# A transformer layer on one core: another order around the last heads, the shared expert and the second batch's first steps

## The reference

```python
x = x + attention(layernorm(x))        # 16 heads, 128 + 64 rotary features per head,
                                       # keys and values from a normed latent of 64
x = x + moe(layernorm(x))              # 8 experts of width 176, each token goes to its top 2;
                                       # beside them a shared expert of width 352
def moe(x):
    scores = softmax(x @ gate_w)                       # decides the experts of a token
    routed = sum over the top 2 of score * (silu(x @ w_gate) * (x @ w_up)) @ w_down
    shared = (silu(x @ sw_gate) * (x @ sw_up)) @ sw_down
    return routed + shared
```

## Time and profile before

| | |
|---|---|
| median of 3 executions | 633.29 us (632.36 to 633.71) |
| the profiled execution | 640.3 us, span 638.6 us |
| TensorE busy | 611.4 us (96%) |
| VectorE busy | 469.9 us (74%) |
| ScalarE busy | 474.8 us (74%) |
| GpSimd busy | 410.1 us (64%) |
| mean granted TensorE clock | 0.974 |

### The profile page before, as it was taken

The page is one execution under the profiler, slowest core; times in us unless marked ns, Lnnn a source line. Parts: engine busy times, 40 slices in busy tenths (PEclk is TensorE's granted clock), DMA queues, the critical chain, the costliest instruction groups (busy, mean ns, idle before and its releaser), DMA issues. The chain is left out here.

```text
span 638.6 us, 15728 instructions
## 1 busy us (share of the span) xinstructions
PE 611.4 (96%) x4916; PEld 596.4 (93%) x4916; DVE 469.9 (74%) x1406; ACT 474.8 (74%) x1331; POOL 410.1 (64%) x455
## 2 busy tenths in 40 slices
PE   9988999999999999999999999999988889999995
PEld 8878999999999999899999999999978879999994
DVE  6666787877886888778688788778755666666486
ACT  4669899898998989779898898979854335565531
POOL 1466797786897889679789988978603204444500
PEclk9997999999999999999999999999989689999997
DMA  9891000000001001000100100011403055444292
GB/s 254 254 332 29 2 1 3 2 2 34 10 10 42 10 18 44 8 16 5 43 18 10 43 9 19 34 53 43 149 1 133 33 152 166 131 119 133 77 316 87
DMA packets 34024, 45.41 MB, mean 71 GB/s; under 512 B 4056, under 2 KB 29112, under 8 KB 33944
## 3 DMA queue, kind: packets, MB, share of 16 engines
q1 hardware_dynamic: 29160, 34.56, 17.2%
q0 software_dynamic: 3408, 9.34, 4.5%
q10 hardware_dynamic: 1376, 0.50, 0.3%
HBM read 27.57 MB, written 16.82 MB: 70 GB/s over the span
## 5 line engine op out<-in xcount | busy, mean ns | idle before, releaser
L1244 ACT ACTIVATE probs<-ps_s,nmax 128x256 f32<-128x256 f32 x256 | 118.9, 475 | 14.4 <-DVE nmax L1434 14.3
L1779 POOL TENSOR_TENSOR qswap<-qswap,qsin 128x512 f32<-128x512 f32 x64 | 83.2, 1300 | 45.6 <-ACT qswap L1221 45.6
L226 PE MATMUL ps_q<-xa,wq_hi 128*128 128x256 f32 x512 | 101.0, 295 | 4.3 <-DVE qf L1429 4.3
L1434 DVE TENSOR_REDUCE nmax<-ps_s 128x2 f32<-128x512 f32 x128 | 86.9, 679 | 11.1 <-PE ps_s L226 10.6
L1221 ACT ACTIVATE pT_hi<-ps_t 128x512 fp32r<-128x512 f32 x128 | 76.6, 598 | 19.6 <-PE ps_t L978 18.2
L1782 POOL TENSOR_TENSOR qf<-qf,qswap 128x512 f32<-128x512 f32 x64 | 82.7, 1293 | 12.9 <-DVE qf L1429 8.9
L1786 POOL TENSOR_TENSOR q_lo<-qf,q_hi 128x512 fp32r<-128x512 f32 x64 | 83.0, 1297 | 6.7 <-ACT q_hi L1221 6.6
L226 PEld LDWEIGHTS ps_q<-xa,wq_hi 128*128 128x128 f32 x512 | 79.9, 192 | 6.0 <-DVE qf L1429 4.0
L299 DVE TENSOR_TENSOR pT_lo<-ps_t,pT_hi 128x512 fp32r<-128x512 f32 x128 | 81.9, 681 | 0.0
L226 PE MATMUL ps_s<-kT_hi,q_hi 128*128 128x256 f32 x256 | 78.3, 306 | 2.1 <-ACT probs L1244 2.1
L978 PE MATMUL ps_t<-ident,probs 128*128 128x128 f32 x512 | 78.0, 275 | 1.3 <-DVE pT_lo L299 1.2
(11 more groups left out here) (337 smaller groups left out, 1924.1 us busy)
## 6 DMA issues: line engine op xcount, KB each, us to landing
xg<-routed_in SPq DMA_DIRECT2D x39, 129.0 KB
normal_turned<-xf SPq DMA_DIRECT2D x8, 512.0 KB, 2.8
wq_raw<-Wq_dram SPq DMA_DIRECT2D x16, 192.0 KB, 4.6
x<-x_dram SPq DMA_DIRECT2D x8, 256.0 KB, 4.9
xa<-normal_turned SPq DMA_DIRECT2D x4, 512.0 KB, 4.8
mgu_hi<-routed_out SPq DMA_DIRECT2D x4, 512.0 KB, 5.2
mgu_lo<-routed_out SPq DMA_DIRECT2D x4, 512.0 KB, 8.0
out_dram<-x SPq DMA_DIRECT2D x8, 256.0 KB, 2.9
```

What stands on the lines that cost most here:

```text
L226: last = nc.tensor.matmul(out, stat, mov, start=start and n == 0, stop=stop and n == len(terms) - 1, skip_group_check=skip)
L1244: last = nc.scalar.activation(probs[h % 3][:, j, :], L.ps_s[h % 2][:, j, :], ACT.Exp, bias=nmax[:, h % NH, j:j + 1], accum_out=rsum[:, h % ...
L1434: vec.tensor_reduce(nmax[:, h % NH, :], L.ps_s[h % 2][:, :, :], AX.X, ALU.max, negate=True).then_inc(ev.max_done, 1)
L1779: gp.tensor_tensor(qs, qs, L.qsin[:, :].unsqueeze(1).to_broadcast([P, 2, S]), ALU.mult).then_inc(ev.qrot_part, 1)
```

## The change

Nothing is added and nothing taken away. Each engine's list has the same instructions in another order, at two places; SyncE's list is the same.

At the front, three steps of batch 1 move from the weights' loop into the first rounds: `prep_moments(1)` behind round 0 on VectorE, `power_a(1)` into round 1 on GpSimd, `prep_normal(1)` into round 1 on ScalarE. Behind the heads, the written-out lists of TensorE, ScalarE and VectorE are in another order, and `gate_up(0, 0)` goes into the last round.

```diff
@@ TensorE @@
                 if pair(g + 4):
                     query(g + 4)
+                if g == PAIRS - 1:
+                    gate_up(0, 0)
                 if pair(g - 1):
                     norms(g - 1)
...
+            gate_up(0, 1)
             turn(HEADS - 1)
-            gate_up(0, 0)
             project(PAIRS - 3)
             norms(PAIRS - 1)
             attend(HEADS - 2)
             attend(HEADS - 1)
             project(PAIRS - 2)
-            gate_up(0, 1)
             gate_up(0, 2)
+            gate_up(1, 0)
             project(PAIRS - 1)
-            rank(B - 2)
-            gate_up(1, 0)
             down(0, 0)
             gate_up(1, 1)
+            rank(B - 2)
             down(0, 1)
             gate_up(1, 2)
             down(0, 2)
             turn_f(B - 1)
             gate_up(2, 0)
+            logits(B - 1)
             down(1, 0)
-            logits(B - 1)
             gate_up(2, 1)
             down(1, 1)
+            gate_up(2, 2)
             rank(B - 1)
-            gate_up(2, 2)
             down(1, 2)
@@ ScalarE @@
-                if h == 15:
-                    prep_normal(1)
...
-                if r == 0 and i >= 1 and batch(i + 1):
+                if (r == 0 and i >= 1 or g == 1) and batch(i + 1):
                     prep_normal(i + 1)
...
             probs_hi(HEADS - 1)
             attended_hi(PAIRS - 2)
+            silu(0, 0)
             norm_out(PAIRS - 1)
-            silu(0, 0)
+            silu(0, 1)
+            unit_hi(0, 0)
             attended_hi(PAIRS - 1)
-            unit_hi(0, 0)
-            silu(0, 1)
             unit_hi(0, 1)
...
-            silu(1, 1)
-            unit_hi(1, 1)
-            for b, m in ((1, 2), (2, 0), (2, 1), (2, 2), (3, 0), (3, 1)):
-                silu(b, m)
-                unit_hi(b, m)
+            silu(2, 0)
+            unit_hi(1, 2)
+            silu(2, 1)
+            unit_hi(2, 0)
+            for n in range(2 * ES + 1, FIRST * ES - 2):
+                silu(*divmod(n + 1, ES))
+                unit_hi(*divmod(n, ES))
             silu(3, 2)
+            unit_hi(3, 1)
@@ VectorE @@
                 if h == 13:
-                    prep_moments(1)
                     maxima(0)
...
+                if g == 0:
+                    prep_moments(1)
...
             units(0, 0)
+            units(0, 1)
+            unit_lo(0, 0)
+            attended(PAIRS - 1)
+            unit_lo(0, 1)
+            units(0, 2)
             masks(B - 2)
...
@@ GpSimd @@
-                if g == 7:
-                    power_a(1)
...
+                if g == 1:
+                    power_a(1)
```

More of the change, by code:

```diff
@@ L1379, in _ @@
             attended_hi(PAIRS - 2)
+            silu(0, 0)
             norm_out(PAIRS - 1)
-            silu(0, 0)
+            silu(0, 1)
+            unit_hi(0, 0)
             attended_hi(PAIRS - 1)
-            unit_hi(0, 0)
-            silu(0, 1)
             unit_hi(0, 1)
+            silu(0, 2)
+            silu(1, 0)
+            unit_hi(0, 2)
+            silu(1, 1)
             split_hi(PARTS + 3)
-            silu(0, 2)
             normal_f(B - 1)
-            unit_hi(0, 2)
-            silu(1, 0)
+            unit_hi(1, 0)
+            silu(1, 2)
             turned_hi(B - 1)
-            unit_hi(1, 0)
+            unit_hi(1, 1)
             nc.scalar.activation(L.warm[:, :], L.one[:, :], ACT.Exp)
             gate_exp(B - 1)
-            silu(1, 1)
-            unit_hi(1, 1)
-            for b, m in ((1, 2), (2, 0), (2, 1), (2, 2), (3, 0), (3, 1)):
-                silu(b, m)
-                unit_hi(b, m)
+            silu(2, 0)
[5 more added lines that the diff above has]
+                unit_hi(*divmod(n, ES))
             silu(3, 2)
+            unit_hi(3, 1)
             rows_hi(0)
@@ L1700, in _ @@
             units(0, 0)
+            units(0, 1)
[3 more added lines that the diff above has]
+            units(0, 2)
             masks(B - 2)
[L1702 to L1705, removed]
+            units(1, 0)
+            unit_lo(0, 2)
             residual(B - 1)
             moments_f(B - 1)
-            unit_lo(0, 1)
-            units(0, 2)
+            units(1, 1)
+            places(B - 2)
+            tokens(B - 1)
+            unit_lo(1, 0)
+            units(1, 2)
             split_lo(PARTS + 3)
-            tokens(B - 1)
-            unit_lo(0, 2)
-            units(1, 0)
             turned_lo(B - 1)
-            unit_lo(1, 0)
             accumulate(0)
+            unit_lo(1, 1)
             gate_max(B - 1)
-            units(1, 1)
-            unit_lo(1, 1)
             masks(B - 1)
-            units(1, 2)
+            units(2, 0)
             unit_lo(1, 2)
-            units(2, 0)
             places(B - 1)
+            units(2, 1)
             unit_lo(2, 0)
             table_counts()
-            units(2, 1)
             accumulate(1)
-            table_tiles()
             unit_lo(2, 1)
             units(2, 2)
-            table_rows()
+            table_tiles()
             unit_lo(2, 2)
             units(3, 0)
+            table_rows()
             unit_lo(3, 0)
+            units(3, 1)
             accumulate(2)
-            units(3, 1)
             unit_lo(3, 1)
+            units(3, 2)
             leave_out()
-            units(3, 2)
             rows_lo(0)
```

## The result

| | before | after |
|---|---|---|
| median of 15 executions each, run side by side | 634.41 us (632.36 to 639.7) | 630.17 us (628.75 to 634.41) |
| the profiled execution | 640.3, span 638.6 | 629.82, span 628.1 |
| TensorE busy, clock | 611.4, 0.974 | 605.3, 0.984 |

The ratio is 0.9929, with a 95% interval from 0.9904 to 0.9953, so 3.0 to 6.1 us faster (ratios are taken over all executions, and can differ a little from what two medians give). On a second chip it was 634.46 to 629.47, 0.992 (0.9897 to 0.9943). The forecast was -6.2 and 627.1. The two profiled executions differ by 10.5 us, more than twice what the medians do, and that gap has to be explained too.

A forecast was written before the change was run, and what follows sets the result against it. A dependency chain from the last attention product to the tables was taken to set when the routed tiles start. Front -1.0 and behind the heads -5.2 made -6.2 us, from 633.29 to 627.1, range 624.0 to 631.0.

The forecast's parts named there:

- steps 1 to 7: Behind the heads, from gate_up(0, 0) in the last round to masks(7): masks(7) at 492.25 instead of 497.82, -5.6 us.
- Step 8: rank(7), behind four shared-expert groups: at 496.3 instead of 501.05, -4.75 us, with 0.65 us of idle.
- the 499 that was named as a sign of being wrong: Behind the heads: rank(7) coming later than 499 us would show the prediction wrong.
- +1.7: Behind the heads: cost in us if one half-clock stretch falls on the attends or on the work ahead of rank(7).
- Steps 9 and 10: From rank(7) to the first routed tile's expert: tables 5.7 us earlier, rows_gate_up(0) at 511.95 instead of 518.85, -6.9.
- I let everything there move with it: Behind the first routed expert at 518.85: no list changes, so all the rest was taken to shift along.
- The front: Weights' loop and first rounds: first maxima 1.34 us earlier, part given back by prep_normal(1); -1.0, bounds -0.2 to -2.1.
- I take the difference unchanged: Whole kernel: the -6.2 us found on the profiled 640.3 us execution was applied to the median 633.29, giving 627.1.
- During the heads TensorE has no gap at all: Heads, from 60 to 125 us: TensorE 65.00 us busy of 65 at full clock.
- The gain eaten by half clock: Rival, behind the heads: half clock behind the new gaps leaves -3.6 us in all, 629.7 us; chance 0.15.
- The dearer table load: Rival, between two ScalarE copies behind the heads: load at twice its 1.28 us, -4.9, 628.4 us; chance 0.04.
- Slower: Rival, behind 511.95: half clock after the wait for the first tile exceeds all gains, 635.1 us at 16 us; chance 0.06.

The follow-up runs named there:

- the clean series: Three kernels on one chip, all with the last masks step moved behind rank's start: before 631.55, edits behind the heads only 629.99, whole change 626.89 us.
- the fill: Changed kernel with gate_up(2, 1) moved ahead of logits(7), from behind down(1, 0), against the kernel before: 625.78 us, ratio 0.9863.
- tail alone: Changed kernel with its three front steps of batch 1 put back, against the kernel before: 628.49 us, ratio 0.9898.
- the second mask's first run: Changed kernel with the last masks step moved from ahead of rank to the head of places(b), against the kernel before: 627.09 us, ratio 0.9877.
- the one clean pair: Two kernels on one chip with the last masks step moved behind rank's start: without the front edits 629.99 us, with them 626.89 us.
- front alone: Kernel before with only the three steps of batch 1 moved into the first rounds, against before: 631.88 us, ratio 0.9949.
- before with the second mask moved: Kernel before with only the last masks step moved behind the point where rank may start, against before: 631.55 us, ratio 0.9930.
- norm first: Changed kernel with ScalarE's norm_out(63) moved ahead of silu(0, 0), against the kernel before: 626.41 us, ratio 0.9875.
- VectorE's units order: Kernel before with silu(1, 1), unit_hi(1, 1) ahead of the exp load and units(1, 1), unit_lo(1, 1) ahead of gate_max(7): 631.07 us, ratio 0.9927.

## Why the prediction was right, and where it was off

- **The number.** 630.17 lies inside the range of 624.0 to 631.0, near its upper end, and 1.2 to 2.0 us of the 6.2 didn't come. The base of 633.29, a median of three, was 1.1 us under the median of 15, so the time is off by more than the difference. That the sum was this near is in part luck: by the medians of the clean series the tail gave 1.6 us where 5.2 were forecast, and the front 3.1 where 1.0 was.
- **The chain, steps 1 to 7**, came out as worked. In old times: attends 475.05 forecast, 475.22 measured; `residual(7)` 482.5 and 482.49; logits 489.95 and 489.89; `masks(7)` 492.25 and 492.64. TensorE's wait for `norm_out(63)` was 2.1 forecast, 2.13 measured.
- **Step 8 was mis-sized for this execution.** `rank(7)` was forecast at 496.3 at full clock, and came at 498.66, near the 499 that was named as a sign of being wrong. The forecast's wait of 0.65 us isn't there; 6.9 us at half clock lay over steps 7 and 8 instead, where +1.7 pays for one stretch of 3.4 us. (The text's "3.4 us of work take twice as long" would be +3.4; +1.7 fits a stretch that lasts 3.4 us.) All seven profiles with the new tail and without the fill have half clock at the logits, six of them for 3.4 us, so the term as priced is the common case. With one stretch ahead of the rank, in tail alone and in the second mask's first run, stage C is 5.5 and 5.1 us shorter than the 71.8 of before, as forecast. The fill, which removes it, gives 3.6 to 4.4 us. Those stretches begin where a gap of 1.04 us is followed by twelve 8-column products, and only then by full work.
- **Steps 9 and 10** held: 9.78 us from rank to the tables' end (9.75), 6.5 from there to the first expert (5.9; half clock again). The first tile is 3.94 us earlier net of the heads, where the forecast's one stretch made it 5.2: 6.9 less 2.36 for step 8, 0.03 for step 9 and 0.57 for step 10.
- **"I let everything there move with it"**, behind 518.85: D is 1.2 us shorter. Before, the first tiles ran at 0.66 (519 to 524). After, the half clock lies ahead of them, from 505, partly in TensorE's wait for the first tile, and the tiles begin at full clock. The windows, of before and of after:

```profile
519.00:524.00 5.00, 5.00 (x24) 4.81 (x25) 2.40 (x8) 1.67 (x5) 0.00 (x0) 0.66 0.71 214
```

```profile
509.60:514.00 4.40, 4.25 (x31) 3.86 (x29) 3.28 (x12) 1.63 (x6) 0.00 (x0) 1.00 0.71 200
```

- **The front**, -1.0: maxima and query came 1.15 us earlier (1.34 and 1.3 forecast), `prep_normal(1)` cost 0.16 us at 63.36. Stage A is 1.7 us shorter on the mean of all profiles, as the half clock there is mostly gone; 3.1 by medians in the one clean pair. The traces are inside the bounds of -0.2 to -2.1, but the value taken was too small.
- **"I take the difference unchanged"** is the step that failed. The sum was made on an execution 7 us over the median, which had two stalls and half clock in stage B and some 13 us of half clock in C; the profiles of the two other kernels with the tail as before (front alone; before with the second mask moved) show C at 70.3 and 69.0 us, not 71.8. Part of the 6.9 us was a bad draw of before, which its median does not have to give. Over all profiles the account closes better: C is 70.3 us on the mean with the old tail (three) and 67.5 with the new one (six, no fill and no norm first), D 119.7 and 118.6, A 36.4 and 34.7. That makes the tail 4.0 us and the front 1.7, 5.7 in all, against 4.2 to 5.0 by the medians. And **"During the heads TensorE has no gap at all"** was read from 60 to 125 us alone; the stalls stood further on in that same trace.
- **Rivals.** The gain eaten by half clock was priced at 629.7, and 630.17 is nearer to it than to 627.1. Its mechanism is in the runs, though not in each execution: half clock at the logits in seven of seven profiles, behind the wait of 2.13 us in three of eight. The dearer table load is refuted (at most 0.02 us on either side of the 1.28 us load). Slower did not come: the stretch at half clock ends with the first tile (1.00 from 509.60).

Open stays what decides in which executions a wait of 1 to 2 us is followed by half clock, and so why front alone and tail alone add up to 10 us and the whole to 4.2 to 5.0. Not tried: the rank ahead of `gate_up(2, 2)`, and VectorE's units order together with the fill or with the second mask moved.

## What to carry to other kernels

Cut two traces at the same instructions and split every stage in idle time and clock before pricing a change; one execution's half clock is a draw, so price from several, or from the fastest. When reordering, look at what stands behind each wait: here full matmuls ahead of 8-column products did better than a gap with the small products behind it. Let a table load never stand ahead of a copy that TensorE waits for. Let no wait of the bounding engine hang on a tiny VectorE step with two SBUF operands beside a busy GpSimd.

## What the runs showed of the hardware

- A 128x16 VectorE instruction with two operands in SBUF took 1.30 us instead of 0.17 when a 1.27 us GpSimd multiplication had begun 0.01 us before, and 0.18 when it began 0.02 us ahead of it. Whether it collides changes from execution to execution. One such stall made stage B 1.1 us longer (364.8 against 363.7), two with a stretch at half clock 3.8. With one operand in PSUM a 128x256 instruction took 0.42 us inside a GpSimd instruction and outside.
- At the same sequence of instructions, two executions of one kernel differ by 5.0 us, 4 of them through TensorE's clock (mean 0.988 and 0.978).
- A gap of 2.10 us in stage A was followed by half clock in five of five profiles, one of 0.87 in three of nine.
- An ACT_TABLE_LOAD between two copies costs its 1.28 us and 0.03 to 0.04 us around it.
